# Node-number rows of a graph kernel's selections moved from SBUF to PSUM, with the PSUM banks rearranged for it

## What is computed

```
def _sage_layer(h, src, dst, W_self, W_neigh, b, n_nodes):
    agg = segment_sum(h[src], dst, n_nodes)
    deg = segment_sum(ones_like(dst), dst, n_nodes)
    return relu(h @ W_self + (agg / maximum(deg, 1.0)[:, None]) @ W_neigh + b)

x = x + sage_layer(sage_layer(layernorm(x), ...1), ...2)
x = x + moe(layernorm(x))      # 8 experts, top 2, each a 512-512-512 network with a norm behind it
```

## Time and profile before

| | |
|---|---|
| median of 3 runs | 2901.69 us (2900.99 to 2908.44) |
| the profiled execution | 2902.25 us |
| its span in the profile | 2900.3 us |
| PE busy | 2395.9 us (83%) |
| POOL busy | 2005.5 us (69%) |
| DVE busy | 1567.2 us (54%) |

### The profile page before, as it was taken

How to read it: one execution, slowest core, us unless ns; L and a number is a source line. 1 busy time by engine, 2 the same in 40 slices (tenths; PEclk the granted TensorE clock), 3 DMA queues, 4 the chain that set the end, 5 groups by cost and what they waited for, 6 DMA issues and landing times.

```text
span 2900.3 us, 55360 instructions
## 1 busy us (share of the span) xinstructions
PE 2395.9 (83%) x11308; PEld 1539.6 (53%) x11309; DVE 1567.2 (54%) x3789; ACT 841.3 (29%) x1611; POOL 2005.5 (69%) x2229
## 2 busy tenths in 40 slices
PE   1188888787888786888888888888988999999996
PEld 0044444444444443455555555554556778888885
DVE  8754454454454443354444444444546677777775
ACT  6512122111211111111111111111114555555554
POOL 0377777777777775777777777777745666666665
PEclk9998898989898999999999999999998999999998
DMA  7679988898987776888888888888875765666543
GB/s 272 231 234 303 303 301 297 298 306 297 312 293 244 231 233 201 277 263 255 257 250 260 255 258 252 259 256 259 261 219 133 162 140 119 141 138 134 106 80 62
DMA packets 239323, 663.61 MB, mean 229 GB/s; under 512 B 47224, under 2 KB 48818, under 8 KB 236168
## 3 DMA queue, kind: packets, MB, share of 16 engines
q0 software_dynamic: 151472, 464.79, 56.4%
q10 hardware_dynamic: 62388, 128.09, 12.4%
q1 hardware_dynamic: 25380, 69.89, 7.5%
HBM read 550.93 MB, written 111.69 MB: 228 GB/s over the span
## 4 chain that ended last, share of the span: by engine, by line
POOL 44%; PE 23%; issue 15%; DMA 11%; DVE 3%; ACT 2%; SPq 1%; POOLq 0%; DVEq 0%; ACTq 0%
POOL store_all L728 43%; PE ps L1767 19%; DMA store_all<-h_scratch,srcT 5%; DMA store_all<-xn_scratch,srcT 4%; PE ps L1932 1%; DMA wts<-expert_weights_scratch 1%; PE ps L1944 1%; ACT store_all L857 1%; SPq L394 1%; ACT ln_out L857 1%; DMA out<-store_all,idx_s 1%; PE ps L1797 1%; PE ps L1798 1%; DMA store_all<-in_L_gnn_W_self 0%; DVE wts L412 0%
## 5 line engine op out<-in xcount | busy, mean ns | idle before, releaser
L728 POOL DMA_INDIRECT store_all<-xn_scratch,srcT x782 | 778.8, 996 | 346.3 <-issue 227.2
L728 POOL DMA_INDIRECT store_all<-h_scratch,srcT x782 | 760.9, 973 | 256.4 <-issue 223.3
L1797 PE MATMUL ps<-store_all,sel 128*128 x1680 | 682.4, 406 | 300.2 <-SPq L616 285.1
L1798 PE MATMUL ps<-store_all,sel 128*128 x1680 | 672.3, 400 | 0.0
L1797 PEld LDWEIGHTS ps<-store_all,sel 128*128 128x128 f16 x1680 | 172.3, 103 | 666.6 <-issue 610.7
L1767 PE MATMUL ps<-wts,sT 128*128 128x512 f32 x1176 | 445.5, 491 | 0.8 <-DVE sT L1369 0.8
L1767 PE MATMUL ps<-wts,aT 128*128 128x512 f32 x1176 | 405.2, 454 | 0.8 <-DVE aT L1375 0.8
L1332 DVE TENSOR_TENSOR sel<-iota_g,dstT 128x384 f16<-128x384 f32 (+2 forms) x602 | 305.8, 525 | 37.5 <-issue 28.7
L1767 PE MATMUL ps<-wts,m_hT 128*128 (+1 forms) x1224 | 313.3, 405 | 4.2 <-DVE m_hT L1643 4.2
L1767 PE MATMUL ps<-wts,m_xT 128*128 (+1 forms) x1224 | 311.6, 403 | 4.9 <-DVE m_xT L1586 3.6
L1767 PEld LDWEIGHTS ps<-wts,sT 128*128 128x128 f32 x1176 | 238.7, 210 | 94.7 <-issue 38.3
(11 more groups left out here) (299 smaller groups left out, 3060.7 us busy)
## 6 DMA issues: line engine op xcount, KB each, us to landing
expert_weights_scratch<-w_both ACTq DMA_DIRECT2D x64, 512.0 KB
wts<-expert_weights_scratch SPq DMA_DIRECT2D x64, 512.0 KB, 4.9
store_all<-in_L_ffn_W ACTq DMA_DIRECT2D x64, 256.0 KB, 5.2
of_experts<-xn_scratch ACTq DMA_DIRECT2D x49, 256.0 KB, 5.3
of_experts<-h_scratch ACTq DMA_DIRECT2D x49, 256.0 KB, 4.1
store_all<-in_x ACTq DMA_DIRECT2D x49, 256.0 KB, 5.2
store_all<-xn_scratch,srcT POOLq DMA_INDIRECT x782, 4.5
store_all<-h_scratch,srcT POOLq DMA_INDIRECT x782, 4.1
```

The lines of the kernel that those rows point to most:

```text
L728: pool.indirect_dma_start(rows[:, t % SLOTS, :], None, rows_d, bass.IndirectOffsetOnAxis(ap=srcT[:, t:t + 1], axis=0)).then_inc(s_rows[t % ...
L1797: pe.matmul(agg_p[p], sel[:, s, :], row[:, 0:D], start=k == 0, stop=False)
L1798: pe.matmul(agg_p[p], sel[:, s, :], row[:, D:2 * D], start=False, stop=False) \
```

## The change

The row of node numbers is kept in PSUM (`nodes_p`): in layer 1 in bank 7, in layer 2 in bank 3, in two halves of 128 columns by parity. Bank 7 held one of the two places for degrees: layer 1 now has one place, in bank 6, and PE's `degrees` waits until DVE has read the degrees of the tile before. Bank 3 held the dense result of odd tiles: in layer 2 both parities now use bank 4, and the bias matmul waits for the `residual` of the tile before instead of the one before that. `iota_g` in SBUF is gone. No instruction is added to or taken from any engine's list, and none changes its place in it, apart from these waits.

```
-            iota_g = sbc(c2, "iota_g", [P, 2, P])
...
-        dense_p = [ps[:, i, :] for i in (4, 3)]
+        dense_p = [[ps[:, i, :] for i in (4, 3)], [ps[:, 4, :]] * 2]
+        nodes_p = [ps[:, i, 0:2 * P].rearrange("p (a n) -> p a n", a=2) for i in (7, 3)]
         agg_p = [ps[:, i, :] for i in range(2)]
-        deg_p = [ps[:, 6 + i, 0:2] for i in range(2)]
+        deg_p = ps[:, 6, 0:2]
...
                 def tile_iota(g, p):
-                    dve.tensor_scalar(iota_g[:, p, :], iota[:], start_col[:, g:g + 1] if isinstance(g, int) else
+                    dve.tensor_scalar(nodes_p[l][:, p, :], iota[:], start_col[:, g:g + 1] if isinstance(g, int) else
...
                     dve.tensor_tensor(
-                        sel[:, s:s + w, :], iota_g[:, p, :].unsqueeze(1).to_broadcast([P, w, P]),
+                        sel[:, s:s + w, :], nodes_p[l][:, p, :].unsqueeze(1).to_broadcast([P, w, P]),
                         dstT[:, bass.ds(t, w)].unsqueeze(2).to_broadcast([P, w, P]), ALU.is_equal) \
...
                 def degrees(g, p):
                     pe.wait_ge(S["seln"], g + 1)
-                    pe.matmul(deg_p[p], sel_n[:, p, :], up_col[:], start=True, stop=False)
+                    if not (isinstance(g, int) and g == 0):
+                        pe.wait_ge(S["rdeg0"], g)
+                    pe.matmul(deg_p, sel_n[:, p, :], up_col[:], start=True, stop=False)
...
                         if k == 0:
-                            if not (isinstance(n, int) and n < 2):
-                                pe.wait_ge(S["res" if l else "relu"], n - 1)
-                            elif l == 0:
+                            if l:
+                                if not (isinstance(n, int) and n == 0):
+                                    pe.wait_ge(S["res"], n)
+                            elif isinstance(n, int) and n < 2:
                                 pe.wait_ge(s_bound, SCALED)
+                            else:
+                                pe.wait_ge(S["relu"], n - 1)
                             pe.wait_ge(s_wset, l + 1)
-                            pe.matmul(dense_p[p], one2[:], bias[l], start=True, stop=False)
+                            pe.matmul(dense_p[l][p], one2[:], bias[l], start=True, stop=False)
```

More of the change, by code:

```diff
@@ L955, in relu @@
                     act.wait_ge(S["store"], n * 16)
-                    act.activation(pair[:, 0:D], dense_p[p], ACT.Relu, scale=sc2[:, 0:1])
-                    act.activation(h_t[:], dense_p[p], ACT.Relu, scale=sc2[:, 0:1]).then_inc(S["relu"], 1)
+                    act.activation(pair[:, 0:D], dense_p[l][p], ACT.Relu, scale=sc2[:, 0:1])
+                    act.activation(h_t[:], dense_p[l][p], ACT.Relu, scale=sc2[:, 0:1]).then_inc(S["relu"], 1)
                 def expert_hi(b, p):
@@ L1346, in degree @@
                     dve.wait_ge(S["node"], g + 1)
-                    dve.tensor_scalar(deg_m[:], deg_p[p][:, 0:1], UP, None, ALU.max).then_inc(S["rdeg0"], 1)
+                    dve.tensor_scalar(deg_m[:], deg_p[:, 0:1], UP, None, ALU.max).then_inc(S["rdeg0"], 1)
                 def count(g, p):
@@ L1388, in residual @@
                     dve.wait_ge(S["xn2"], n)
-                    dve.scalar_tensor_tensor(out=x2_t[:], in0=dense_p[p], scalar=0.0, in1=x_t, op0=ALU.max,
+                    dve.scalar_tensor_tensor(out=x2_t[:], in0=dense_p[l][p], scalar=0.0, in1=x_t, op0=ALU.max,
                                              op1=ALU.add).then_inc(S["res"], 1)
@@ L1794, in sums @@
                     if l == 0 and k == ST:
-                        pe.matmul(deg_p[p], sel[:, s, :], up_col[:], start=False, stop=False)
+                        pe.matmul(deg_p, sel[:, s, :], up_col[:], start=False, stop=False)
                     row = slot_of(t)
@@ L1802, in degrees @@
                     pe.wait_ge(S["seln"], g + 1)
-                    pe.matmul(deg_p[p], sel_n[:, p, :], up_col[:], start=True, stop=False)
+                    if not (isinstance(g, int) and g == 0):
+                        pe.wait_ge(S["rdeg0"], g)
+                    pe.matmul(deg_p, sel_n[:, p, :], up_col[:], start=True, stop=False)
                 def closing(g, p):
                     if l == 0:
-                        pe.matmul(deg_p[p], zero2[:], zero_row[:, 0:2], start=False, stop=True)
+                        pe.matmul(deg_p, zero2[:], zero_row[:, 0:2], start=False, stop=True)
                     pe.matmul(agg_p[p][:, 0:2], zero2[:], zero_row[:, 0:2], start=False, stop=True).then_inc(S["node"], 1)
@@ L1840, in step @@
                             pe.wait_ge(S["aggLo"], n + 1)
-                        i = product(dense_p[p], wts[l][:, 1 - k // KC], sT if k < KC else aT, (k % KC,), k == 2 * KC - 1)
+                        i = product(dense_p[l][p], wts[l][:, 1 - k // KC], sT if k < KC else aT, (k % KC,), k == 2 * KC - 1)
                         if k == KC - 1:
```

## The result

| | before | after |
|---|---|---|
| median | 2901.49 us (2900.68 to 2908.44, 6 runs) | 2865.61 us (2863.70 to 2871.87, 6 runs) |
| profiled execution | 2902.25 us, span 2900.3 | 2870.31 us, span 2868.4 |
| ratio, 95% interval | | 0.9875 [0.986, 0.989] |

The kernel is faster by 1.25%, 36 us between the medians and 31.9 us between the two profiled executions. The forecast was 29 us, 2873, in a range of 2864 to 2888.

The account below looks back on a forecast made before the run. POOL's back-to-back gathers (line 728) were taken as the bound. From 2902.25 us, 29 came off, the middle of 23.2 to 35.5, other costs being 0; with the median 0.56 lower, 2872.7, rounded 2873, range 2864 to 2888.

Parts of the forecast that it names:

- The bound: POOL's gathers, line 728: POOL runs without a stop, one gather each 1.25 us, with slots always free in time.
- Selections: With node numbers in PSUM, 35.5 us of delays to 144 gathers behind selections go; a gather needs something 0.13 us after starting.
- What comes back: Freed gathers can be caught by DVE lines 1382, 1365, 1499 and 1500, leaving a gain between 23.2 and 35.5 us.
- the 6.5 taken with no row to decide: Delay assumed to return at those DVE lines, implied by taking 29 us, the middle between gains of 23.2 and 35.5.
- the 0 to 12.3: Range of returning delay in us: none if the phases stay, 12.3 if gathers meet the remaining DVE lines at any phase.
- The signs that were named: Line 728's mean falls from 996 and 973 ns to about 975 and 956, with some 22 and 8 us left.
- the step that lets line 1500 meet gathers at any phase: Line 1500, 98 rows with a hold of 0.40 us, costs 6.3 us and holds up more gathers than now.
- DVE: DVE's own time: 0 to +8 ns per selection, line 1312 up to 311 ns more; hidden beside other work, cost 0.
- The sum: Profiled 2902.25 us less 29 gives 2873.25; runs' median is 0.56 lower, so 2872.7, in round figures 2873.
- No gain: Rival, chance 0.06: something merely coinciding with selections lengthens the gathers, which get no faster; 2902 us.
- Less than half: Rival, chance 0.10: gathers issued faster do not land faster, the DMA engines rising to 0.89 busy; 2887 or 2893 us.
- Slower by phase: Rival, chance 0.04: remaining DVE rows come again and again at the same bad moment of a gather; 2920 us at 70%.

Follow-up runs that it names:

- the banks only: Changed kernel's new PSUM places and two new PE waits, but node numbers kept in SBUF: 2907.29 us beside 2907.03 for the kernel before, 1.0001.

## Why the prediction was right, point by point

*The bound.* Right: the last column above is the test. POOL stayed the bound, slots stayed free, PE kept a wait of 258.7 us for rows. One sign that was named, line 728 at the head of the chain, can't be read from the first profile of the changed kernel: its chain that ended last gives PE 21% and POOL 0%, so it wasn't followed back into the layers. The other two profiles of that kernel have POOL at 44% of their chains.

*Selections.* Right in the cause: no gather behind a selection is held any more, and with the numbers back in SBUF 165 are. But the moment was misread. What counts is not which row runs 0.13 us into a gather, but which row has begun when the gather starts. Before the change, 153 gathers started while a selection was running that had more than 0.145 us to go; 144 of them were held, and of the nine others eight started less than 0.04 us behind the selection. In 44 gathers a selection began within the first 0.125 us and no earlier row stood there: none of these was held. Here is one, where the selection runs until 1907.30, 0.63 us into the gather:

```profile
1906.67 0.95 POOL L728 DMA_INDIRECT store_all<-h_scratch,srcT  x1 [0.30 <-SPq L626]
1906.74 0.56 DVE L1332 TENSOR_TENSOR sel<-iota_g,dstT 128x384 f16<-128x384 f32 x1
```

With the banks only the same counts are 165 of 185 and none of 33. The 0.13 us is then how far ahead of the row's recorded end a held gather goes on; whether the row lets go that early, or the gather has other work first, stays open. The page "SBUF — State Buffer" of the Trainium skill, section "Who interferes with whom", has both rules that were weighed: the one on two SBUF operands agrees with these runs where DVE's row is first (144 gathers held before, none after), the remark that `tensor_tensor` does not hold up GpSimd's DMAs does not. That the one which starts first keeps the read side for the whole instruction does not hold here where the gather is first: the 384-column selections that began 0.04 to 0.125 us behind a gather's start took their usual 553 ns on the mean.

*What comes back.* Right in its size, and that by luck. In the three profiles 5.0, 4.2 and 5.8 us came back (35.5 less the fall of the delay from 60.2), for the 6.5 taken with no row to decide. But neither layer lies in the middle of the 0 to 12.3. In layer 1 the phase is any: lines 1382 and 1365 cost 23.3, 17.8 and 23.5 us, against the working's 16.6 + 7.1 = 23.7. In layer 2 it is not: lines 1499 and 1500 cost 0.4 to 0.8 us, against 6.3 + 2.0. Before, the two pairs cost 17.7 and 1.5 us. So 0 to 6 us came back in layer 1, and in layer 2 another 1 went. The signs that were named show it: 975 and 956 ns were expected, some 22 and 8 us left, and the profile has 983 and 947, 28.9 and 0.8. The two misses cancel in the sum.

What failed here is the step that lets line 1500 meet gathers at any phase and hold up more of them than before; it held 8 and now 1 to 3. The reason is in the timelines: its rows now begin just behind a gather's start, where they hold nothing. Before, the row had begun 0.04 us or more ahead of the start of 8 gathers, and held all 8; 13 began between that and 0.125 us behind the start, and held none on their own. In the three profiles of the changed kernel these numbers are 1, 3 and 4 gathers, of which 1, 2 and 3 were held, and 34, 33 and 30. Why DVE's rows fall just there was not tried.

*DVE.* Right in its cost of 0. The selections' price came out at -2 ns, outside the bounds of 0 to +8; line 1312's at +42 ns, inside.

*The sum.* 60.2 - 29.7 = 30.5 us of delay went in the profiled executions, and the time fell by 31.9; forecast 29. The medians are 34 to 36 us apart on the three occasions. On the first this is more than between the profiles because the profiled execution of the changed kernel was one of its slower ones, 4.7 us above its median, and that of the kernel before only 0.8. The prediction was worked out from a single execution, and the delay of one kernel differs from execution to execution; the range held that.

*The rivals.* No gain: excluded. Less than half: excluded, with the DMA engines at 0.87 and 0.83 of the two layers where 0.89 was feared. Slower by phase: its mechanism is real (the delay of one kernel differs by several us between executions), but the rows that could have locked badly in layer 2 locked well, just behind the gathers' starts, which nothing in the prediction foresaw.

## What to carry to other kernels

Where indirect DMAs from POOL run back to back and set the pace, look at what DVE is already running when each one starts. Rows with two SBUF operands lengthened the gathers here without showing in any wait; moving one operand to PSUM, or cutting the longest such row into pieces, gave that time back even where DVE itself got slower. Ask then what the sooner gathers run into: here it was the space of the raw weights.

## What the runs showed of the hardware that was not expected

The blocking goes both ways. In layer 2 of the changed kernel 24 of the 98 rows of line 1499 are longer than 330 ns, and all of these end 0.047 to 0.053 us after a gather's end; 19 of the 98 of line 1500 are longer than 500 ns, and end 0.187 to 0.195 after one. All of them began 0.5 us or more behind the gather's start. Rows that began less than 0.49 us behind it, 29 and 33, took 286 and 486 ns at the most. The timeline above has a long one: line 1500 at 1651.17 runs until 1651.79, the gather until 1651.61. So these rows, with one SBUF tensor and an SBUF result, wait for the end of a gather in whose later part they begin, while lines 1332 and 1365 keep their 551 and 682 ns within it. It was so before the change too, with 33 rows of line 1499 and 3 of line 1500. Whether these waits bring the next rows to their place just behind a gather's start was not tried.

A PSUM operand cost a selection nothing (551 ns after 553), and an ACT result written to PSUM instead of SBUF was somewhat quicker (653 ns after 679 at 512 columns, line 957).
